# Folding the score weights, tiling the scores by columns and moving four z tiles in the front of a graph network kernel

## The reference

```python
z = jnp.einsum('ni,hoi->nho', h, Wfc)
s_src = jnp.einsum('nho,ho->nh', z, a_src)
s_dst = jnp.einsum('nho,ho->nh', z, a_dst)
e = jax.nn.leaky_relu(s_src[src] + s_dst[dst], negative_slope=NEG_SLOPE)
m = jax.ops.segment_max(e, dst, num_segments=N)
ex = jnp.exp(e - m[dst])
denom = jax.ops.segment_sum(ex, dst, num_segments=N)
alpha = ex / denom[dst]
out = jax.ops.segment_sum(alpha[:, :, None] * z[src], dst, num_segments=N)
```

## Time and profile before

| | us |
|---|---|
| median of 3 runs (3441.39 to 3456.38) | 3445.44 |
| the profiled execution | 3450.27 |
| its span, first to last instruction | 3448.6 |
| layer 0: scores, z and picks, scans to the transposes | 21.1, 92.6, 349.4 to 467.2 |
| layer 1: the same | 1958.0, 2029.1, 2259.2 to 2386.5 |
| mean granted clock of PE, as a share of 2.4 GHz | 0.918 |

### The profile page before, as it was taken

How to read it: one execution, slowest core, us unless ns; L and a number is a source line. 1 busy time by engine, 2 the same in 40 slices (tenths; PEclk the granted TensorE clock), 3 DMA queues, 4 the chain that set the end, 5 groups by cost and what they waited for, 6 DMA issues and landing times. The chain is left out here.

```text
span 3448.6 us, 37641 instructions
## 1 busy us (share of the span) xinstructions
PE 2910.2 (84%) x8976; PEld 1407.9 (41%) x8977; DVE 2013.8 (58%) x3553; ACT 654.5 (19%) x1088; POOL 1560.9 (45%) x1504
## 2 busy tenths in 40 slices
PE   5979888888887883399999499977989889684998
PEld 2445332222233553255555245533223222283665
DVE  7665846666665886723332356576666666666554
ACT  2000320000002661011111120013111111261333
POOL 4671037777772000134443137301777777402565
PEclk9989989999999885599999799999999999857999
DMA  7356357777773112045555567424777777546776
GB/s 232 93 98 162 117 155 209 210 209 209 209 210 107 74 73 92 22 111 149 144 143 149 139 144 136 127 81 142 211 210 211 210 211 211 149 176 181 125 123 110
DMA packets 344052, 523.72 MB, mean 152 GB/s; under 512 B 173155, under 2 KB 178643, under 8 KB 343263
## 3 DMA queue, kind: packets, MB, share of 16 engines
q0 software_dynamic: 115872, 317.04, 36.5%
q1 hardware_dynamic: 100335, 200.76, 17.8%
q10 hardware_dynamic: 127696, 4.06, 2.1%
HBM read 435.01 MB, written 86.70 MB: 151 GB/s over the span
## 5 line engine op out<-in xcount | busy, mean ns | idle before, releaser
L1095 POOL DMA_INDIRECT aggregate_zg<-z_rows,src_groups x940 | 892.1, 949 | 502.4 <-issue 274.8
L1168 PE MATMUL bank<-aggregate_zg,aggregate_onehot 128*128 x1888 | 945.8, 630 | 119.3 <-DVE aggregate_zg L1138 111.8
L1138 DVE TENSOR_TENSOR aggregate_zg<-aggregate_zg,bank 128x1024 f32<-128x1024 f32 x470 | 573.6, 1220 | 429.5 <-DMA aggregate_zg<-z_rows,src_groups 429.1
L1168 PEld LDWEIGHTS bank<-aggregate_zg,aggregate_onehot 128*128 128x128 f32 x1888 | 312.2, 191 | 751.3 <-issue 739.2
L737 PE MATMUL bank<-alpha,front_table 128*120 128x512 bf16 x1152 | 287.1, 386 | 14.7 <-DVE alpha L618 14.7
L1803 POOL DMA_INDIRECT exp_xg<-hn_rows,exp_gather_tok x64 | 71.7, 1120 | 499.4 <-DVE exp_gather_tok L1865 378.1
L1078 ACT ACTIVATE acc<-bank 128x512 f32<-128x512 f32 x60 | 35.9, 598 | 1087.1 <-PE bank L1168 1087.1
L416 POOL DMA_INDIRECT front_d<-src_scores,src_chunks x192 | 195.1, 1016 | 94.6 <-issue 58.2
L737 PEld LDWEIGHTS bank<-alpha,front_table 128*120 128x120 bf16 x1152 | 154.8, 135 | 189.8 <-issue 104.2
L318 PE MATMUL bank<-front_w,x 128*128 128x512 f32 x480 | 219.6, 617 | 12.8 <-ACT front_edge L326 10.9
L1947 PE MATMUL bank<-exp_w,exp_h_t 128*117 128x512 f32 x512 | 225.7, 595 | 0.7 <-ACT exp_h_t L1894 0.7
(11 more groups left out here) (425 smaller groups left out, 3507.2 us busy)
## 6 DMA issues: line engine op xcount, KB each, us to landing
exp_w<-in_L_ffn_w SPq DMA_DIRECT2D x32, 1024.0 KB, 7.3
x<-x_rows SPq DMA_DIRECT2D x10, 1536.0 KB, 15.2
aggregate_zg<-z_rows,src_groups POOLq DMA_INDIRECT x940, 3.7
x<-in_x SPq DMA_DIRECT2D x8, 1536.0 KB, 14.2
front_edge<-src_key SPq DMA_DIRECT2D x32, 384.0 KB, 3.6
front_edge<-src_tile SPq DMA_DIRECT2D x32, 384.0 KB, 3.5
front_early<-src_key SPq DMA_DIRECT2D x32, 384.0 KB, 3.5
front_early<-src_tile SPq DMA_DIRECT2D x32, 384.0 KB, 3.6
```

Source lines behind the costliest of these rows:

```text
L1095: pool.indirect_dma_start(zg[:, r, j, :], None, k.z_rows[:, :], bass.IndirectOffsetOnAxis(k.src_groups[:, n:n + 1], 0)).then_inc(gathered[ ...
L1138: v.tensor_tensor(z, z, bcast_last(scales[:, at:at + J * H], DH), ALU.mult).then_inc(msg_ready, 1)
L1168: mm = nc.tensor.matmul(k.banks[:, bass.ds(bank, 1), :].rearrange("p a n -> p (a n)"), onehot_at(n)[:, j, :], zg[:, bass.ds(at, 1), j, :]. ...
```

## The change

1. The weights of the scores are folded on PE. SP loads `w` a second time in rows of its outputs (`w_rows`, into `d`), and a matrix of 512 by 16 made on the host from `a_src` and `a_dst`, which has a head's weights in the column of that head. PE multiplies them (16 products), ACT copies the result to `wa`, which now has 32 columns per quarter of the features, 16 of them zero.
2. The four products of a score group no longer add up: each writes its own 32 partitions. ACT copies all 128, and the turning back multiplies with `unstack`, which adds the four.
3. The count of edge groups is made on PE: POOL writes a row of node numbers, DVE compares it with the last destinations (120 partitions, two columns), PE sums over partitions in 60 products of one column, and DVE takes the result after its first statistics. DVE's statistics now run a block ahead of its normalising.
4. Six z tiles stand behind the scores, with slots 2 and 3 and three banks; ACT issues their stores. Before its first pick DVE waits until they are stored. `w` itself is loaded after the third block of the input.
5. Three slots for rows of keys and tiles instead of two.
6. The bounds are made in 16 parts, every third pick from 35; the steps of the tables stand a little further apart; `load_dst` stands before `take_sums(0)`.
7. In the scans PE projects in quarters of a tile (`UNITS_TO`).

```diff
-Z0 = 2
+Z0 = 6
+ROW_SLOTS = 3
-STEPS_AT = (18, 20, 23, 26, 29)
-BOUNDS_AT = (33, 36, 39, 42)
+STEPS_AT = (18, 21, 25, 27, 29, 33)
+PEN_PARTS = 4
+BOUNDS_AT = tuple(range(35, 35 + 3 * 4 * PEN_PARTS, 3))
-Z_BEFORE = ((2, 5, 4, 5, 3), (2, 7, 3, 5, 3))
+UNITS_TO = ((10, 33, 47, 69, 83), (9, 37, 51, 76, 90))
...
+        z_bank = lambda n: k.ps[(6, 7, 4)[n % 3] if n < Z0 else (6, 7, 4, 5)[(n - Z0) % ZS]]
+        z_slot = lambda n: 2 + n % 2 if n < Z0 else (n - Z0) % ZS
...
                 load_x(0)
-                sp.dma_start(w[:, :, :], w_dram.rearrange("(c p) n -> p c n", p=P)).then_inc(loaded, 16)
-                sp.dma_start(a_b[:, 0, :], a_src_dram.partition_broadcast(P)).then_inc(loaded, 16)
-                sp.dma_start(a_b[:, 1, :], a_dst_dram.partition_broadcast(P)).then_inc(loaded, 16)
+                sp.dma_start(w_out, w_rows.rearrange("(c p) n -> p c n", p=P)).then_inc(heads_loaded, 16)
+                sp.dma_start(heads, a_heads.rearrange("(c p) n -> p c n", p=P)).then_inc(heads_loaded, 16)
                 load_x(1)
                 if layer == 0:
                     sp.dma_start(src_i, I["src_list"].rearrange("(p n) -> p n", p=P)).then_inc(src_loaded, 16)
+                load_x(2)
+                sp.dma_start(w[:, :, :], w_dram.rearrange("(c p) n -> p c n", p=P)).then_inc(loaded, 16)
...
+                    if r == 2:
+                        sp.wait_ge(s_turned, NSG)
+                    if r >= ROW_SLOTS:
+                        sp.wait_ge(onehot_ready, (r - ROW_SLOTS + 1) * PB)
...
-                for n in range(Z0):
-                    store_z(sp, n)
...
+                    nc.gpsimd.iota(node_row, pattern=[[1, NPAD]], base=0, channel_multiplier=0, allow_small_or_imprecise_dtypes=True).then_inc(rows_listed, 1)
...
-                    for t in range(NT):
-                        ins = v.tensor_scalar(less[:, t, 0:NG], lasts, k.node[:, t:t + 1], 0.0, ALU.is_lt, ALU.add, accum_out=group[:, t:t + 1])
+                    dve.wait_ge(rows_listed, 1)
+                    for a in range(J):
+                        v.tensor_scalar(later_node[0:GP, a, :], node_row[0:GP, :], lasts[0:GP, a:a + 1], None, ALU.is_gt).then_inc(lasts_compared, 1)
...
                 stats(0)
+                if layer == 0:
+                    take_groups()
                 norm(0)
                 stats(1)
-                norm(1)
-                dve.wait_ge(loaded, 48)
-                for s in range(2):
-                    chain(v.tensor_tensor(prod, w[:, :, :], a_b[:, s, :].unsqueeze(1).to_broadcast([P, KC, D]), ALU.mult))
-                    ins = v.tensor_reduce(wa[:, :, s * H:(s + 1) * H], prod.rearrange("p c (h d) -> p c h d", h=H), AX, ALU.add)
-                for b in range(2, NT // SBT):
-                    stats(b)
-                    if layer == 0 and b == 2:
+                for b in range(1, NT // SBT):
+                    if b + 1 < NT // SBT:
+                        stats(b + 1)
+                    if layer == 0 and b == 1:
                         split_sources()
                     norm(b)
...
-                for u in range(2, min(Z0, ZS)):
-                    dve.wait_ge(z_stored[u], 16 * len(range(u, Z0, ZS)))
+                for u in range(2, ZS):
+                    dve.wait_ge(z_stored[u], 16 * z_times(u, Z0))
...
-                        mm = nc.tensor.matmul(k.ps[2 + g % 2][0:2 * H, 0:len(tiles) * P], wa[:, c, :], hn_t(c, slice(tiles[0], tiles[-1] + 1)),
-                                              start=(c == 0), stop=(c == KC - 1))
+                        mm = nc.tensor.matmul(k.ps[2 + g % 2][c * SH:(c + 1) * SH, 0:len(tiles) * P], wa[:, c, :], hn_t(c, slice(tiles[0], tiles[-1] + 1)),
+                                              start=True, stop=True)
...
-                        mm = nc.tensor.transpose(k.ps[5][:, n * 2 * H:(n + 1) * 2 * H], s_t[:, g % 2, j * P:(j + 1) * P], k.ident[0:2 * H, 0:2 * H])
+                        mm = nc.tensor.matmul(k.ps[5][:, n * 2 * H:(n + 1) * 2 * H], s_t[:, g % 2, j * P:(j + 1) * P], unstack, start=True, stop=True)
...
+                pe.wait_ge(heads_loaded, 32)
+                for c in range(KC):
+                    for o in range(KC):
+                        mm = nc.tensor.matmul(k.ps[4][:, c * 2 * H:(c + 1) * 2 * H], w_out[:, o, c * P:(c + 1) * P], heads[:, o, :], start=(o == 0), stop=(o == KC - 1))
+                mm.then_inc(wa_made, 1)
+                if layer == 0:
+                    pe.wait_ge(lasts_compared, J)
+                    for t in range(NT):
+                        for a in range(J):
+                            mm = nc.tensor.matmul(k.ps[7][:, t:t + 1], later_node[0:GP, a, t * P:(t + 1) * P], ones_bf[0:GP, 0:1], start=(a == 0), stop=(a == J - 1))
...
+                act.wait_ge(wa_cleared, 1)
+                act.wait_ge(wa_made, 1)
+                nc.scalar.copy(wa[:, :, 0:2 * H], k.ps[4][:, 0:KC * 2 * H].rearrange("p (c n) -> p c n", c=KC)).then_inc(wa_ready, 1)
                 root(0)
...
                     take_z(act, n)
+                    store_z(act, n)
...
                 for m, (kind, n) in enumerate(turn_order):
-                    if m == halfway:
-                        take_sums(0)
                     if (kind, n) == ("d", 0):
                         act.wait_ge(scattered, 16 * NT)
                         for r in range(DR):
                             load_dst(r)
+                    if m == halfway:
+                        take_sums(0)
...
-                    for t in range(projected(n - 1) if n else Z0, projected(n)):
-                        project(pe, t)
+                    for t, c in units[units_to[n]:units_to[n + 1]]:
+                        project(pe, t, c)
```

More of the change, by code:

```diff
@@ L284, in front @@
         d_loaded = [sem(f"d_loaded{r}") for r in range(DR)]
-        keys_loaded, tiles_loaded = ([sem(f"{n}_loaded{u}") for u in range(2)] for n in ("keys", "tiles"))
+        keys_loaded, tiles_loaded = ([sem(f"{n}_loaded{u}") for u in range(ROW_SLOTS)] for n in ("keys", "tiles"))
         onehot_ready, selected, mask_done, block_done = sem("onehot_ready"), sem("selected"), sem("mask_done"), sem("block_done")
@@ L572, in make_bounds @@
                 def make_bounds(step):
+                    which, part = step // PEN_PARTS, step % PEN_PARTS
+                    lo, n = part * (CL // PEN_PARTS), CL // PEN_PARTS
+                    here = dst[:, 1 + lo:1 + lo + n]
                     if step == 0:
@@ L677, in _ @@
                 turn_scores(NSG - 1)
+                pe.wait_ge(loaded, 16)
+                if layer == 0:
+                    pe.wait_ge(groups_ready, 1)
                 for n in range(Z0):
-                    if n == ZS - 1:
-                        pe.wait_ge(s_copied, 2)
-                    project(pe, n)
+                    for c in range(KC):
+                        project(pe, n, c)
                 def side_work(m):
@@ L829, in front @@
         ag = av.rearrange("p c g j h -> p (g j) c h")
-        projected = lambda n: Z0 + sum(Z_BEFORE[layer][0:n + 1])
+        units = [(n, c) for n in range(Z0, NT) for c in range(KC)]
+        units_to = (0,) + UNITS_TO[layer] + (len(units),)
+        projected = lambda n: Z0 + units_to[n + 1] // KC
         def take_back(copy, u):
@@ L859, in _ @@
                 for u in range(ZS):
[L860 removed]
+                    sp.wait_ge(z_stored[u], 16 * z_times(u, NT))
             if layer == 0:
@@ L1002, in _ @@
                     nc.tensor.matmul(k.ps[1][:, 0:CH], k.head_sel_t[:, :], shifted, start=True, stop=True).then_inc(from_pe, 1)
-                for t in range(projected(4), NT):
-                    project(pe, t)
+                for t, c in units[units_to[5]:]:
+                    project(pe, t, c)
                 pe.wait_ge(z_copied, NT)
@@ L2415, with by_head @@
     by_group = lambda v: v.reshape(CH, GC, J, P).transpose(3, 0, 1, 2).reshape(P, -1)
+    def by_head(*parts):
+        rows = np.zeros((D, len(parts) * H), parts[0].dtype)
+        for n, part in enumerate(parts):
+            for h in range(H):
+                rows[h * DH:(h + 1) * DH, n * H + h] = part.reshape(H, DH)[h]
+        return rows
     by_chunk = lambda v: v.reshape(CH, GC, J, P).transpose(3, 1, 2, 0).reshape(P, -1)
```

142 lines of the change are left out of this document (78 added, 64 removed).

## The result

The changed kernel takes 3410.4 us, median of four runs (3406.1 to 3414.0), against 3450.9 for the kernel before on the same chip: a ratio of 0.988 (95% interval 0.985 to 0.992). It is faster by 40 us. The forecast was 3396, 14 us less, with a range of 3375 to 3420. The profiled execution took 3413.96 us with a span of 3412.2, so 36.4 of span are gone against the earlier trace rows.

A forecast was written before the change was run, and what follows sets the result against it. PE was taken to pace scores and layer 0's picks, z the scans, DMA loads layer 1's picks. Terms +8 -29 -21.8 +6.5 -12.5 = -49 took 3450.3 us to 3401; the median lying 4.9 lower, 3396, range 3375 to 3420.

The forecast's parts named there:

- Picks: Layer 0's pick stage: stalls on DVE and ACT mostly go, 249.0 us becomes 220, -29 us.
- Scans: Layer 0's scans: fewer z tiles, in quarters, so transposes start at 444.2 instead of 467.3; -21.8 us.
- Layer 1's scans: Layer 1's scans: exponentials end at 2372.5, transposes start at 2374 instead of 2386.5; -12.5 us.
- I take 2.15: Scores: us for one score group of four matmuls in four column groups, between bounds of 0.9 and 3.6.
- the staircase: Score group: a pass overlaps only with the first of the next matmul, five steps instead of eight.
- Counting is 60 passes ... I take 6: Layer 0's scores: PE's count in 60 one-column passes takes 6 us, from a range of 6 to 13.
- The turning back: Scores: turning a score group back on PE, priced at 0.4 us per four tiles.
- picks at 2045.1: +6.5 (... +3.5 to +9): Layer 1: key rows and last z store land at 2044.4 behind SP's crowded queue; picks start 6.5 us later.
- (1): Rival: column groups overlap fully, 0.9 us a group, layer 1 gaining until the row loads bind; 3386 us, 25%.
- (2): Rival: column groups do not overlap, 3.6 us a group, 9 us later in each layer; 3414 us, 15%.
- (3): Rival: layer 0's picks keep half of their stalls; 3410 us, 8%.
- (4): Rival: slower, each score pass waits for the one before to drain; 3491 us at 8.5 us a group, 3%.

The follow-up runs named there:

- e5: Changed kernel with layer 0's run bounds made in 4 whole parts again instead of 16 quarters; 3415.5 us, ratio 0.989.
- e6: Changed kernel with layer 0's first d loads issued behind ScalarE's copies of the first sums again; 3411.9 us, ratio 0.990.
- e4: Changed kernel with smaller portions of layer 1's z work behind the picks (9, 24, 39, 64, 80 of 96 units); 3405.7 us, ratio 0.985.
- e7: Changed kernel with layer 1's two lists sent as one DMA each instead of 32 DMAs of 8 rows; 3386.1 us, ratio 0.981.
- e2: Changed kernel with two z tiles ahead of layer 1's picks and the earlier kernel's portions behind them; 3424.2 us, ratio 0.991.
- e11: Changed kernel with the two lists' DRAM tensors declared ahead of all other inputs, program unchanged; 3409.5 us, one run.
- e3: Changed kernel with the scores back in one group of 32 columns, all column groups undone; 3434.5 us, ratio 0.994.
- e10: Changed kernel with layer 1's lists as one DMA each and the scores in one column group again; 3425.5 us, ratio 0.991.
- e12: Changed kernel with layer 1's lists as one DMA each and portions at 9, 24, 39, 64, 80 units; 3375.5 us, ratio 0.976.

## Why the prediction was right or wrong

**The direction and the range were right**, and so was most of layer 0. Picks: 220 forecast, 222.0 measured, with the loads issued at 176 (188 to 206 forecast); e5 and e6 show both causes named, 12 and 9 us. Scans: -21.8 forecast, -21.1 measured (96.7 us from PE's first z tile behind the picks to the transposes, 117.9 before); PE's z ends with ACT's last exponentials (416.5 and 416.3 us), nearly ahead of them as forecast, but 2.3 of DVE's 2.7 us carry wait stayed, where I had taken 2.3 off. That the sum fits even so is in part luck: the 1.3 us set against it, for the last x reload, are not in this stretch, since that load goes out at 418.62, behind the transposes' start. Layer 1's scans: -12.5 forecast, -12.2 measured; the transposes start 1.0 us behind the last exponential, which ends 3.8 us later in the stretch than before, where 3 were forecast. What the forecast left out there is the wait of 11.75 us at the second carry that the kernel before already had: e4 gets 7 us out of it.

**Two prices of layer 0's scores were too high.** "I take 2.15" for a score group: it is 1.06, and the staircase on which it rested does not exist; the lower bound, 0.9, was near. "Counting is 60 passes ... I take 6": 1.74, 29 ns a pass. The row of narrow float32 passes was far from bf16 passes of one column. The fold was 7.01 for 7.0. It is not the count that holds the first normalisation, as I had put it, but ACT's root, behind the copy of the fold and two table loads of 1.28 us on ACT, which I had not counted:

```profile
26.15 0.19 DVE L480 RECIPROCAL rstd<-front_d 128x6 f32<-128x6 f32 x1 [1.34 <-ACT front_d L804]
```

The turning back was priced too low, 1.06 us for 0.4. In all, the first normalisation starts at 26.4 instead of 30.4, z at 72.9 instead of 82.5, the picks at 98.3 instead of 107.5. Layer 0 gained 49.0 where 42.8 were forecast.

**The step that failed is layer 1's "picks at 2045.1: +6.5 (... +3.5 to +9)".** Measured +20.8 (109.0 against 88.2). The place was right, rows and last z store behind a crowded SP queue, and the sum took for granted that the queue moves as before plus half a megabyte. It did not see what the crowd was. The earlier trace rows show DVE waiting for src_key; the 10.76 us for et_by_kind just ahead of that, shown above, have no part in the sum, and they end with the lists. The DMA share of 0.91 in the earlier trace rows does not say how much moves: a share near 1 goes with 137 GB/s beside the pieces and with 405 behind them in e7. The lists went through 8 DMA engines in 32 pieces one after the other, and in the changed kernel a piece took 1.87 us instead of 1.49: 32 times 0.38 is 12 us of the 14 by which the term was short; the packets' whole stretch grew by 14, from 49 to 63 us. e7 shows that the lists set the start, e2 that the z stores are worth 2.4 of it. Why a piece became slower stays open (e11).

**The rivals.** (1) held in its mechanism: the groups overlap fully. Its time, 3386, did not come, since the lists swallowed layer 1's share (e3 against e10: 1.4 and 20.2 us); "until the row loads bind" was the right condition, with a binding far tighter than I put it. (2), (3) and (4) did not happen: no score group over 1.94 us (the first of each layer; in layer 1 the granted clock was 0.50 there), and in layer 0's picks no stall over 0.95 us behind the first pick. The rule cited against the change, the drain at a change of tiling mode in the Trainium skill's "TensorEngine Tiling (Array Packing)", Key Properties, leaves no gap that the rows above show: transposes, score group and turning back start 1.05, 0.99 and 0.92 us apart. The one for it, in "TensorE: Matmul & The Clock Gate", Part 3, Measured speedup vs the span model, agrees: 2.38 times there for three groups, 3.61 over 1.06, or 3.4 times, here for four.

So the total came out 14 us high: layer 0 gave 6 more, layer 1 took 16 more, some 3 are the scatter of a stretch that the change leaves alone, and 1 is that the profiled execution lay 3.6 us above its median and not 4.9.

## What to carry to other kernels

When a stage gets shorter, look up what was hidden behind it, also in the queue that it doesn't use: DVE's wait for layer 1's lists ended 1.4 us before PE was through with the scores, and once those were quick the lists cost 24 us. A DMA share near 1 does not tell how many bytes move; here it went with 137, 218 and 405 GB/s. Count how many packets are in flight at once, and try a broadcast with an outer dimension that 16 engines can share, as in e7. And a portion of filler work on an in-order engine must end where its buffers do, or the small urgent step behind it waits for a buffer.

## What the runs showed of the hardware

- Eight float32 passes in four column groups of 32, of 512 columns each, take 1.06 us at the higher clock and 3.62 in one group (e3): the groups run side by side, and 1.06 us is little more than two passes of 0.45 us (3.62 over 8), so the two of a group seem to follow each other.
- A list packet of 15,360 bytes takes 1.49 to 1.94 us with 8 of them in flight, and 1.11 to 1.13 with 16 (e7 to e10, e12). Other transfers are slower beside the pieces too: in the changed kernel run_bounds' packets of 7,680 bytes took 0.94 us on average while they were under way and 0.29 afterwards (packet records). What the two share stays open. That the 8 rows of a piece all read the same bytes may matter; that wasn't tried.
- A matmul of one bf16 column takes 29 ns with its own weights (60 in 1.74 us; the clock isn't on record there).
- 28 z units planned, but PE stops after 30 passes (15 units) when ACT is held up: the banks, not PE, set how much filler work fits ahead of a carry (11.76 us of stall). In e4, with 15 units planned, PE stands as long (12.80), but for DVE's carry, which it then serves at once.
